# Second attention of a decoder: sums combined ahead of the gates, scores scaled and negated in the bias add

## What is computed

```python
q = query @ q_w + q_b; k = query @ k_w + k_b; v = query @ v_w + v_b
q = q * hd ** (-0.5) / 32                       # 16 heads of 8
k = concatenate([k, tile(bias_k)]); v = concatenate([v, tile(bias_v)])   # one more key
attn_weights = einsum('bth,bsh->bts', q, k)
pb = rel_emb[relative_bucket]                   # position bias by head
gate = sigmoid((q_unscaled @ grep_w + grep_b).sum(-1)) * grep_a
probs = softmax(attn_weights + gate * pb)
attn = einsum('bts,bsh->bth', probs, v)
x = layernorm(x + attn @ out_w + out_b)
```

## Time and profile before

| | |
|---|---|
| median of 3 runs | 4137.38 us (4135.95 to 4141.83) |
| profiled execution | 4147.94 us, its span 4146.2 us |
| instructions | 92196 |
| busy over the whole span | PE 3539.4, DVE 3134.3, ACT 2357.5, POOL 1846.6 us |
| second self-attention | from about 1600 to 2490 us of the span |
| costliest groups there | ACT exp L1824 326.2 us (x1024), POOL posg L1652 266.3 (x256), PE turn L1731 227.2, DVE maximum L1936 177.0, DVE bias add L1934 172.6 |

### The profile page before, as it was taken

The page is one execution under the profiler, slowest core; times in us unless marked ns, Lnnn a source line. Parts: engine busy times, 40 slices in busy tenths (PEclk is TensorE's granted clock), DMA queues, the critical chain, the costliest instruction groups (busy, mean ns, idle before and its releaser), DMA issues. The chain is left out here.

```text
span 4146.2 us, 92196 instructions
## 1 busy us (share of the span) xinstructions
PE 3539.4 (85%) x30917; PEld 2304.7 (56%) x30917; DVE 3134.3 (76%) x6483; ACT 2357.5 (57%) x5257; POOL 1846.6 (45%) x2322
## 2 busy tenths in 40 slices
PE   6899999997675863988999886888759999999998
PEld 3466666664445762666666665777624444444443
DVE  6677777775764654888888885888868888888887
ACT  1455555555672443777777774656545555555555
POOL 1000000002553653556565652222237878787876
PEclk9999999998886875677777777888879999999999
DMA  2000000001112211000000002222165666666664
GB/s 79 7 10 10 10 10 10 10 9 32 46 44 76 66 35 33 16 15 14 15 13 15 15 8 54 57 56 55 46 166 136 139 135 140 133 143 133 136 137 87
DMA packets 279448, 243.73 MB, mean 59 GB/s; under 512 B 57832, under 2 KB 205324, under 8 KB 279308
## 3 DMA queue, kind: packets, MB, share of 16 engines
q1 hardware_dynamic: 267916, 237.21, 24.1%
q10 hardware_dynamic: 11392, 4.79, 0.5%
HBM read 210.34 MB, written 31.59 MB: 58 GB/s over the span
## 5 line engine op out<-in xcount | busy, mean ns | idle before, releaser
L2651 POOL TENSOR_TENSOR d_hidden<-d_gated,d_upper 128x512 f32<-128x512 f32 x528 | 802.7, 1545 | 228.5 <-DVE d_upper L2760 103.5
L2767 DVE TENSOR_TENSOR d_h_low<-d_hidden,d_h_high 128x512 f16<-128x512 f32 x528 | 540.7, 1024 | 119.1 <-ACT d_h_high L2727 117.9
L2721 ACT ACTIVATE d_gated<-d_g 128x512 f32<-128x512 f32 x528 | 315.4, 597 | 461.4 <-PE d_u L2667 461.4
L750 POOL MEMSET f_minus_half<- 128x4 f32 x1 | 0.1, 103 | 866.5 <-POOLq L37 866.5
L2760 DVE TENSOR_TENSOR d_upper<-d_u,d_coef 128x512 f32<-128x512 f32 x512 | 349.3, 682 | 29.0 <-DMA d_coef<-coefT 10.3
L2727 ACT ACTIVATE d_h_high<-d_hidden 128x512 f16<-128x512 f32 x528 | 328.4, 622 | 8.1 <-POOL d_hidden L2651 8.1
L1824 ACT ACTIVATE c_sc<-c_sc,c_negmax 128x129 f32<-128x129 f32 x1024 | 326.2, 393 | 11.7 <-issue 7.7
L1652 POOL TENSOR_TENSOR c_posg<-w_pos,c_gate 128x512 f32<-128x512 f32 x256 | 266.3, 1041 | 0.0
L2665 PE MATMUL d_g<-d_x_high,w_Wg_high 128*128 128x512 f16 x528 | 200.5, 380 | 73.2 <-POOL d_x_low L2644 37.3
L1829 ACT ACTIVATE c_pT<-c_turned 128x512 f32<-128x512 f32 x256 | 149.8, 585 | 156.1 <-PE c_turned L1731 155.9
L1731 PE MATMUL c_turned<-all_ident,c_sc 128*128 128x128 f32 x1024 | 227.2, 361 | 8.2 <-ACT c_sc L1824 7.4
(11 more groups left out here) (409 smaller groups left out, 9900.6 us busy)
## 6 DMA issues: line engine op xcount, KB each, us to landing
d_coef<-coefT SPq DMA_DIRECT2D x256, 512.0 KB, 7.3
d_cT<-in_ctxT SPq DMA_DIRECT2D x128, 64.0 KB, 2.0
mx_x<-in_xT SPq DMA_DIRECT2D x16, 256.0 KB
b_x<-in_x SPq DMA_DIRECT2D x64, 64.0 KB
y<-b_y SPq DMA_DIRECT2D x64, 64.0 KB, 1.6
f_y<-y SPq DMA_DIRECT2D x16, 256.0 KB, 3.3
f_x<-in_x SPq DMA_DIRECT2D x16, 256.0 KB, 3.8
x<-f_res SPq DMA_DIRECT2D x16, 256.0 KB, 2.4
```

The lines of the kernel that those rows point to most:

```text
L2651: nc.gpsimd.tensor_tensor(hidden[b][:], gated[b][:], upper[b][:], ALU.mult).then_inc(h_ready, 1)
L2721: nc.scalar.activation(gated[b][:], ps_g[i][:], ACT.Silu, scale=1.0 / W_SCALE).then_inc(silu_ready, 1)
L2767: nc.vector.tensor_tensor(h_low[b][:], hidden[b][:], h_high[b][:], ALU.subtract).then_inc(h_low_ready, 1)
```

## The change

The position biases are made times -1 in place of divided by SCALE (setup). The bias add and the add for the last key become one instruction each that multiplies the PSUM operand by -SCALE and adds the bias. What stands in sc is thus minus the scaled score; a row's minimum over it is minus the scaled maximum, and is itself the bias of the exp, whose scale becomes -1.0. The multiplication L1938, the tensor `top` and the wait of DVE on its own reduce (the Own counter `quarters_own`) go. On PE, combine comes ahead of gates_and_values.

```diff
-                nc.vector.tensor_scalar(relb[:], rel[:], 1.0 / SCALE, None, ALU.mult).then_inc(relb_ready, 1)
+                nc.vector.tensor_scalar(relb[:], rel[:], -1.0, None, ALU.mult).then_inc(relb_ready, 1)
...
                         run(turn_x, ahead2)
+                        run(combine, behind2)
                         run(gates_and_values, ahead1)
-                        run(combine, behind2)
...
-                        last = nc.scalar.activation(sc[s][:, h, :], sc[s][:, h, :], ACT.Exp, bias=negmax[s][:, h:h + 1], scale=SCALE)
+                        last = nc.scalar.activation(sc[s][:, h, :], sc[s][:, h, :], ACT.Exp, bias=negmax[s][:, h:h + 1], scale=-1.0)
...
-                    nc.vector.tensor_tensor(sc[s][:, :, T].rearrange("p (a i) -> p i a", a=4), gates_part(1), by_gate(last_bias[s]), ALU.add).then_inc(gate_done, 1)
+                    nc.vector.scalar_tensor_tensor(sc[s][:, :, T].rearrange("p (a i) -> p i a", a=4), gates_part(1), -SCALE, by_gate(last_bias[s]),
+                                                   ALU.mult, ALU.add).then_inc(gate_done, 1)
...
-                    nc.vector.tensor_tensor(sc[s][:, hs, 0:T], sbank[a % 2][:], posg[a][:], ALU.add).then_inc(biased, 1)
+                    nc.vector.scalar_tensor_tensor(sc[s][:, hs, 0:T], sbank[a % 2][:], -SCALE, posg[a][:], ALU.mult, ALU.add).then_inc(biased, 1)
                     dve.wait_ge(biased, quarter(it, j, a))
-                    m = own.mark(nc.vector.tensor_reduce(top[s][:, hs], sc[s][:, hs, :], AX, ALU.max))
-                    own.wait(m)
-                    nc.vector.tensor_scalar(negmax[s][:, hs], top[s][:, hs], -SCALE, None, ALU.mult).then_inc(top_ready, 1)
+                    nc.vector.tensor_reduce(negmax[s][:, hs], sc[s][:, hs, :], AX, ALU.min).then_inc(top_ready, 1)
```

More of the change, by code:

```diff
@@ L1515, in phase_attn1 @@
         sc, pT = slots("sc", [T, H, KEYS]), slots("pT", [T, H, T])
-        top, negmax, den = slots("top", [T, H]), slots("negmax", [T, H]), slots("den", [T, H])
+        negmax, den = slots("negmax", [T, H]), slots("den", [T, H])
         attn, attnT, y, res = slots("attn", [T, H, HD]), slots("attnT", [D, T]), slots("y", [T, D]), slots("res", [T, D])
@@ L1528, in phase_attn1 @@
                  "lastT_ready", "lastT_copied", "pv_ready", "attn_ready", "attnT_ready", "attnT_copied", "out_ready", "x_biased_ready", "x_added", "mv_ready",
-                 "rstd_ready", "offset_ready", "x4_ready", "own_front", "var_ready", "gate_added", "gate_ready", "last_bias_ready", "gate_inverted", "own_quarters", "own_back", "waited", "pool_waited", "low_ready", "rhs_ready", "chosen_ready", "weighed_ready", "weighed_copied")
+                 "rstd_ready", "offset_ready", "x4_ready", "own_front", "var_ready", "gate_added", "gate_ready", "last_bias_ready", "gate_inverted", "own_back", "waited", "pool_waited", "low_ready", "rhs_ready", "chosen_ready", "weighed_ready", "weighed_copied")
         (consts, xT_ready, xT_copied, qvk_ready, vlast_ready, whole_ready, high_ready, rows_ready, misc_ready, gate_exp, v_ready,
@@ L1532, in phase_attn1 @@
          lastT_ready, lastT_copied, pv_ready, attn_ready, attnT_ready, attnT_copied, out_ready, x_biased_ready, x_added, mv_ready,
-         rstd_ready, offset_ready, x4_ready, own_front, var_ready, gate_added, gate_ready, last_bias_ready, gate_inverted, own_quarters, own_back, waited, pool_waited, low_ready, rhs_ready, chosen_ready, weighed_ready, weighed_copied) = (ph.sem(n) for n in names)
+         rstd_ready, offset_ready, x4_ready, own_front, var_ready, gate_added, gate_ready, last_bias_ready, gate_inverted, own_back, waited, pool_waited, low_ready, rhs_ready, chosen_ready, weighed_ready, weighed_copied) = (ph.sem(n) for n in names)
         def nth(it, j):
@@ L1883, in _ @@
             def _(dve):
-                front_own, quarters_own, back_own = Own(dve, own_front), Own(dve, own_quarters), Own(dve, own_back)
+                front_own, back_own = Own(dve, own_front), Own(dve, own_back)
                 dve.wait_ge(consts, 1)
@@ L1924, in last_score @@
                     dve.wait_ge(v_ready, nth(it, j))
-                    nc.vector.tensor_tensor(sc[s][:, :, T].rearrange("p (a i) -> p i a", a=4), gates_part(1), by_gate(last_bias[s]), ALU.add).then_inc(gate_done, 1)
+                    nc.vector.scalar_tensor_tensor(sc[s][:, :, T].rearrange("p (a i) -> p i a", a=4), gates_part(1), -SCALE, by_gate(last_bias[s]),
+                                                   ALU.mult, ALU.add).then_inc(gate_done, 1)
                 def bias(it, j, a):
-                    s, own, hs = slot(j), quarters_own, slice(4 * a, 4 * a + 4)
+                    s, hs = slot(j), slice(4 * a, 4 * a + 4)
                     if a == 0:
-                        own.step(place(it, j))
                         dve.wait_ge(gate_done, nth(it, j))
```

## The result

The changed kernel has a median of 4011.15 us (4007.77 to 4014.41, 4 runs) against 4138.85 us before (4 runs): a ratio of 0.9692 with an interval of 0.9677 to 0.9706, so 127.7 us less. The profiled execution took 4014.4 us, its span is 4012.6.

The account below looks back on a forecast made before the run. No engine was full in the second attention, so a loop between engines set the pace. DVE's view gave 11.5 us a column, PE's 12.0; the larger counted: (13.45 - 12.0) x 64 = 93 us saved, median 4044, range 3985 to 4100.

Parts of the forecast that it names:

- the forecast's own 4015 to 4075: Whole kernel: range of the main forecast, median 4044, chance 0.62.
- signs of being wrong: Bias adds at 0.77 or more, stage's mean clock outside 0.65 to 0.85, or L1914 waiting for POOL's low parts.
- short column: Second attention: the column of 12.93 us becomes 10.8 us, DVE's own bound.
- (1): DVE, second attention: removing L1938 saves 0.18 us a quarter, 0.36 for two such quarters.
- (2): DVE, fourth quarter: removing L1938, which lasts 0.66 us beside POOL's L1652, saves 0.65 us.
- (3): DVE, first quarter: without L1938 and L1944's 0.65 us wait for PE, the short column saves 1.12 us.
- the wait of L1944 goes with the order: PE, second attention: combining ahead of the gates leaves DVE's wait at L1944 near zero.
- no large wait: PE, second attention: the gates no longer wait long for POOL's L1636.
- my bounds 0 to +0.1 us: DVE bias add as a two-operation instruction: bounds on added time each, with +0.01 us taken.
- PE as a bound: PE, second attention: at a mean clock of 0.72, one column per 12.0 us if PE never waited.
- rival A: Clock goes high for nearly the whole second attention: column 10.9, 163 us saved, median 3974; chance 0.15.
- long column: Second attention at the low clock: column becomes 12.8 us, with the projection on PE late.

Follow-up runs that it names:

- Experiment 1: Kernel before with only combine moved ahead of gates_and_values on PE: 4057.55 us, ratio 0.9811.
- experiment 7: Changed kernel, but each quarter's minimum goes to its own tensor and a second 4-element reduce copies it to negmax: 4038.02 us, ratio 0.9759.
- experiments 6: Changed kernel with 64 increments, plus one unread f32 matmul of 256 columns per attention column ahead of the combining: 3962.37 us, ratio 0.9571.
- experiment 9: Changed kernel with the old order on PE, plus two unread f32 matmuls per attention column ahead of the gates: 4081.64 us, ratio 0.9861.
- Experiment 8: Kernel before with only the new PE order, plus one unread f32 matmul per attention column ahead of the combining: 4062.54 us, ratio 0.9813.
- 64 increments: Changed kernel with 64 semaphore increments that compute nothing added on DVE ahead of the last phase: 3989.05 us, ratio 0.9633.

## Why the prediction was right, and which step was not

The measured 4011 us lie in the stated range of 3985 to 4100, but below the forecast's own 4015 to 4075, and one of its signs of being wrong came true: the stage's mean clock is 0.91. What DVE gains was right; the step that turned it into a time was not.

**Right: what L1938 is worth.** I had 10.8 us for the short column; it is 10.61, and DVE has hardly a gap in it. The step from the reduce to the next instruction is 0.61 us, not 0.65, four times a column: 0.16 of the 0.19 us. Experiment 1 against the changed kernel isolates the term. Steps (1), (2) and (3) without its 0.65 of wait sum to 0.36 + 0.65 + 0.47 = 1.48 us; measured 12.18 - 10.62 = 1.56. That POOL's L1652 held L1938 up was only argued in the prediction; experiment 7 and the rows there show it, with L1620 as the one that does it in the first quarter. The page named there (the Trainium skill, SBUF — State Buffer, section Who interferes with whom) has it that a tensor_reduce never contends: the trace agrees, 157 ns in the mean where the multiplication took 363.

**Right: the wait of L1944 goes with the order, at no new wait.** 78.7 us fell to 5.9 with the order alone and 12.5 with both. The gates' wait for POOL fell from 67.8 to 7.7 us though I had foreseen only "no large wait". The bias add's median is 679 ns in both kernels, so of my bounds 0 to +0.1 us the lower held. The combining was done 2.9 us after the row transpose (foreseen 2.7) and DVE reached L1943 3.02 after it (foreseen 3.1), so the wait is gone by a narrow margin. ACT (9.97 of 10.61 us busy) and POOL (8.10) took the new pace; L1915 waited for POOL's low parts 6.5 us in 7 times, not a bound.

**Failed: "PE as a bound".** I held the clock's mix of levels at 0.72 and made a floor of 12.0 us a column from it, and let that decide: saved 93 us. The stage gave 159. The columns have a mean of 10.97 us ((2295.38 - 1614.97) / 62 from transpose to transpose), and the stage's mean clock, 0.91, went out of my range of 0.65 to 0.85. That is rival A, 163 us, to which I had given 0.15. Two things were wrong in the step. First, the mix is an outcome of the loop, not a property of the stage. Before, PE stood waiting 67.8 us for POOL's L1636; with both edits it does more matmuls per us (6019 against 4854 in the same 640 us, in part an effect of the clock itself) and the level stays high. That giving PE more to do raises the clock is shown by experiments 6 and 9, where only matmuls were added that nobody reads: 0.93 to 1.00 between 1640 and 2280 us, 27 us less; 0.79 to 0.95, 54 us less. The Trainium skill (TensorE: Matmul & The Clock Gate, section What's actually happening) says "activity releases the throttle"; the trace agrees by these numbers. The added matmuls also stand where PE had been waiting (the gates' wait fell from 59.4 to 29.0 us in experiment 9), so these runs do not part the work from the shorter gap; experiment 1, with the gap closed and the clock at 0.77, speaks against the gap alone. Second, the formula was no use as a forecast even at a fixed mix: with the order alone the clock was 0.77, the floor by my own formula 1 / (0.54 / 9.8 + 0.46 / 14.5) = 11.5 us, and DVE's 12.18 the larger. It gives a floor that was never the one met. In time: the stage gave 66 us more than the 93, the last phase took 31 back, and 128 is what was left.

**Size of the long column.** Where the level is low, a column takes 12.29 us (clock 0.64), and DVE waits at L1899 for the projection, as foreseen, 15.7 us in 17 times. I had 12.8 and expected a third of the columns to be long; only four of 63 take 12.3 and eight 11.7, by the clock again.

**Missed: the last phase.** Nothing in the prediction looked at an untouched stage. The cost is 31 us in the profiles and 22 between medians (4011.15 - 3989.05). It cancelled part of my error: without it the time is 3989, 55 us from my 4044 and 15 from rival A's 3974; with it my 4044 stands 33 us from 4011. That it came as near as this is luck, two errors of opposite sign. The range would still have held 3989, by 4 us.

**How the parts join.** By the ratios the order alone gives 78 us; the arithmetic alone 5, or 36 with the stall of 31 taken out of it; both, stall taken out, 128 + 31 = 159. Together they give 45 us more than their sum. The stage's lengths in the profiles give 80, 47 and 159, so 32 more. So there is a surplus, of some 30 to 45 us. Experiment 9 (the arithmetic with two) says why for the arithmetic: at a low clock its time goes into the wait for the combining, and at a high one the old order still costs 1.5 us a column. Experiment 8 (the order with one) says it for the order: without the arithmetic DVE is the bound, and a higher clock is worth nothing to it. The order frees PE, the arithmetic DVE, and each alone stops at the other.

**Open.** What exactly lets the level rise or fall is not settled, nor why the kernel before turned a higher clock into only 6 us. That the stalls are loads of code is inferred, closely: from their place at the loop's start, the 25 packets more, a packet 2.3 to 2.5 us ahead of the end of each stall, and their coming and going by a shift. The exact place of the boundary is known only as lying between 32 and 64 increments, and that 192 more act like some 64 fewer was tried at this one distance.

## What to carry to other kernels

Cost a removed instruction by the step from its start to the next one's, and ask which engine works beside it: an instruction of 0.17 us at its shortest was worth 0.39 us on the mean here (1.56 / 4). A clock that depends on the engine's work belongs on the side of the results: where an edit closes gaps on PE, give the case with the high clock a sum of its own and much of the chance. A little useless work on PE is worth a try where the low level makes turns of the loop longer: it gave 27 and 54 us so, 6 in the kernel before, and nothing where DVE set the pace at either level. When a phase that the diff does not touch changes while the busy times of most of its engines don't, look for idle time put down to nothing at a loop's start and for packets of the code queue in it, and shift the code.

## What the runs showed of the hardware that I had not expected

A loop's time depends on where its code lies. 72 DVE instructions fewer far ahead of the last loop made DVE stand five times for 5.6 us on the mean (28.2 us) and the phase 31 us longer; 64 dummies brought it back, 32 did not, and 192 in the kernel before brought the same stall. The Trainium skill (Runtime: NRT & Kernel Launch, section Instruction fetch mechanics) says that a taken branch to code outside the window held on the engine forces a load before the engine goes on; the trace agrees, with a stall of up to 5.91 us at the loop's start each time it goes round, a packet of instruction code 2.4 us before its end, and 45 such packets in the phase against 19 with the 64 increments. The size of that window no run here shows.

PE stayed at the low level through 14 us without a gap. In the changed kernel one more f32 matmul of 256 columns per column of some 11 us, read by nobody, kept it at the high level and made the kernel 27 us faster.

L1938, a tensor_scalar of 128x4 on DVE, waited for POOL: all its 127 long cases in the kernel before end 0.02 to 0.03 us after an instruction of POOL, and from 0.17 us it went up to 1.07. A tensor_reduce of the same size in the same place took 156 to 160 ns in all 256 cases, though half of them start beside a running instruction of POOL.
